# Norm sums and products on GpSimd, second block's head outputs moved by DMA, last projections in four banks

## What is computed

```python
h = _layer_norm(x, scale, offset)              # over the 512 columns
qh = (h @ wq + bq); kh = (ctx @ wk + bk); vh = (ctx @ wv + bv)      # 16 heads of 128
kh, vh = concatenate([kh, bias_k]), concatenate([vh, bias_v])       # 361 keys + 1
weights = softmax(qh @ kh.T / sqrt(128)); x = x + (weights @ vh) @ wo + bo
...
x = x + gelu(_layer_norm(x) @ w_fc1 + b_fc1) @ w_fc2 + b_fc2        # 512 -> 2048 -> 512
```

## Time and profile before

| | |
|---|---|
| median of 3 runs | 2356.04 us (2351.41 to 2356.37) |
| the profiled execution | 2354.95 us, span 2353.2 us |
| busy share of the span | PE 94%, PE weight load 92%, DVE 69%, ACT 51%, POOL 37% |
| granted TensorE clock, mean | 0.978 |
| first block's attention | about 0 to 1662 us of the span |
| its MLP | about 1662 to 1823 us |
| second block's attention | about 1823 to 2197 us |
| its MLP | about 2197 to 2353 us |

### The profile page before, as it was taken

The page is one execution under the profiler, slowest core; times in us unless marked ns, Lnnn a source line. Parts: engine busy times, 40 slices in busy tenths (PEclk is TensorE's granted clock), DMA queues, the critical chain, the costliest instruction groups (busy, mean ns, idle before and its releaser), DMA issues.

```text
span 2353.2 us, 37111 instructions
## 1 busy us (share of the span) xinstructions
PE 2219.7 (94%) x12712; PEld 2154.2 (92%) x12712; DVE 1635.1 (69%) x3781; ACT 1189.4 (51%) x2902; POOL 874.2 (37%) x854
## 2 busy tenths in 40 slices
PE   6999989999998999999899999989999899888899
PEld 5999989999998999999899999988898788877899
DVE  7777777776777777777777777766464776677543
ACT  4545554554555455554554555544232576576332
POOL 4324323242431414334142432413799112211487
PEclk9999999999999999999999999999999999999999
DMA  3646545554554546455454555534444211100143
GB/s 131 139 83 146 106 99 98 116 122 101 131 111 87 129 86 146 101 111 133 76 123 82 147 107 116 121 73 77 125 113 121 72 46 56 46 20 19 50 122 112
DMA packets 127255, 235.40 MB, mean 100 GB/s; under 512 B 22753, under 2 KB 64865, under 8 KB 127073
## 3 DMA queue, kind: packets, MB, share of 16 engines
q1 hardware_dynamic: 127072, 233.03, 44.4%
HBM read 214.96 MB, written 4.92 MB: 93 GB/s over the span
## 4 chain that ended last, share of the span: by engine, by line
PE 74%; DVE 13%; ACT 4%; POOL 4%; issue 3%; DMA 1%; SPq 0%; DVEq 0%; POOLq 0%; ACTq 0%
PE bank L693 71%; PE bank L765 2%; POOL mring L650 2%; DVE U L1294 2%; DVE ctxN L1298 1%; POOL mring L648 1%; PE bank L951 1%; DVE pT L1298 1%; ACT qT L1077 1%; DVE prob L1461 1%; ACT U L1077 1%; DVE kT L1294 1%; DVE lnb L1339 1%; DVE tmp L1408 1%; DVE ctxT L1298 1%
## 5 line engine op out<-in xcount | busy, mean ns | idle before, releaser
L648 POOL TENSOR_SCALAR mring<-stage 128x512 fp32r<-128x512 f32 x325 | 229.2, 705 | 1221.2 <-PE bank L693 1077.1
L693 PE MATMUL bank<-ctxT,kring 128*128 128x362 f32 x3456 | 632.7, 330 | 3.6 <-DVE ctxT L1298 3.6
L693 PEld LDWEIGHTS bank<-ctxT,kring 128*128 128x128 f32 x3456 | 585.9, 190 | 8.6 <-POOL mring L650 3.7
L693 PE MATMUL bank<-pT,ctxN 128*128 128x400 f32 (+1 forms) x2304 | 475.3, 354 | 12.9 <-DVE U L1298 12.8
L650 POOL TENSOR_TENSOR mring<-stage,mring 128x512 fp32r<-128x512 f32 x325 | 436.3, 1343 | 27.1
L693 PEld LDWEIGHTS bank<-pT,ctxN 128*128 128x128 f32 (+1 forms) x2304 | 419.3, 192 | 14.6 <-issue 14.4
L693 PE MATMUL bank<-hT,mring 128*128 128x400 f32 x1608 | 319.1, 347 | 13.7 <-POOL mring L650 5.8
L693 PE MATMUL bank<-U,mring 128*128 128x400 f32 x1536 | 313.0, 357 | 5.6 <-POOL mring L650 3.7
L693 PEld LDWEIGHTS bank<-hT,mring 128*128 128x128 f32 x1608 | 294.6, 189 | 18.7 <-issue 8.8
L693 PEld LDWEIGHTS bank<-U,mring 128*128 128x128 f32 x1536 | 281.6, 193 | 8.8 <-POOL mring L650 5.2
L1298 DVE TENSOR_TENSOR U<-bank,U 128x400 fp32r<-128x400 f32 x256 | 146.0, 572 | 172.6 <-ACT U L1077 172.6
(11 more groups left out here) (90 smaller groups left out, 2973.5 us busy)
## 6 DMA issues: line engine op xcount, KB each, us to landing
ctxT_raw<-in_ctx SPq DMA_DIRECT2D x72, 724.0 KB, 7.4
ctxN_raw<-in_ctx SPq DMA_DIRECT2D x256, 192.0 KB, 3.1
stage<-in_wk SPq DMA_DIRECT2D x64, 256.0 KB, 4.3
stage<-in_wq SPq DMA_DIRECT2D x64, 256.0 KB, 2.7
stage<-in_wv SPq DMA_DIRECT2D x64, 256.0 KB, 3.7
stage<-in_wo SPq DMA_DIRECT2D x64, 256.0 KB, 2.7
stage<-in_fa SPq DMA_DIRECT2D x64, 256.0 KB, 2.7
stage<-in_fb SPq DMA_DIRECT2D x64, 256.0 KB, 2.6
```

The costliest lines, as they stand in the source:

```text
L648: nc.gpsimd.tensor_scalar(hi, src, 1.0, 1.0, ALU.mult, ALU.mult).then_inc(S.w_hi, 1)
L693: mm = pe.matmul(dst, parts_l[a], parts_r[b], start=first and k == 0, stop=last and k == len(order) - 1)
```

## The change

- Norms 1 to 4, 7 and 8: the two sums go to POOL, as does the product with the reciprocal; the product with the column scale goes to ACT (`norm_scale` there). Differences, squares, high and low parts are cut into two pairs of chunks and put in neighbouring steps; the reciprocal is cut into halves of 200 columns. The norm then ends at n0+9 instead of n0+6. (For norm 7, the first sum stays on DVE.)
- Norm 0: PE adds the four chunks itself in `first_mean` and `first_var`.
- Second attention: `value_sum1_high` and `value_sum1_low` copy the whole bank, 128 x 400, into `heads_out` (the buffer of the second query tile), and SP moves it to `attnT` with four DMAs (`save_heads`). ACT waits for them (`at_in`) before it writes `heads_out` again, and `project1` waits for them. The queries of half 1 use one buffer and come a step later.
- The last group's projections use four banks (`o_bank`), with no wait for x between them; `up(1)` comes ahead of them, and in the second MLP ahead of `project1`.
- The four "1v" tiles are loaded by DMAs of their own and split by ACT and DVE in F = 13 to 17.

```diff
-        add(275 + 6 * j, "1v", j)
         add(T_MLP[0] + NF - 1 + j // 2, "1q", j)
         add(303, "1k", j)
-        add(T_ATT1 + 9 + j, "1c", 0, j)
+        add(T_ATT1 + 10 + j, "1c", 0, j)
         add(T_ATT1 + 29, "1c", 1, j)
...
-IN_W1 = {("a", 1): 0, ("b", 0): 1, ("a", 2): 2, **{("1v", j): j for j in range(4)},
-         **{("1c", 1, j): j for j in range(4)}}
+IN_W1 = {("a", 1): 0, ("b", 0): 1, ("a", 2): 2, **{("1c", 1, j): j for j in range(4)}}
...
+BY_POOL = [1, 2, 3, 4, 7, 8]
...
-        attnT = qT
+        attnT, heads_out = qT, qs[1]
 
         bank = [ctx.enter_context(nc.psum_tensor(f"bank{i}", [P, 512], F32)) for i in range(8)]
         M_BANK, T_BANK = 5, 4
         U_BANK = [6, 7]
         V_BANK = [5, 6, 7, 5]
+        O_LAST = [5, 6, 7, 4]
...
+        def qs_of(Q):
+
+            if Q < 4:
+                return Q % 2, 32 * (Q // 2)
+            return 0, 64 + 32 * (Q - 4)
+
+        def o_bank(G, c):
+            return bank[O_LAST[c] if G == GN - 1 else M_BANK]
...
         APPLIED = [[], [], [0, 1, 2], []]
-        S_CPROJ, CPROJ = NS // 2 + 3, [[0], [1], [2, 3], []]
-        S_Q1 = 8
+        S_CPROJ, CPROJ = NS // 2 + 3, [[], [0], [1, 2, 3], []]
+        S_Q1 = 9
...
+            def save_heads(t):
+
+                b, j = divmod(t, 4)
+                sp.wait_ge(S.y_lo, t + 1)
+                for i in range(HG):
+                    r, a = slice(i * HD1, (i + 1) * HD1), j * ROWS + b % NB * LQ
+                    sp.dma_start(f32(attnT[r, :, a:a + LQ]), f32(heads_out[r, :, i * LQ:(i + 1) * LQ]))\
+                        .then_inc(S.at_in, 16)
+
+            def load_values_weight():
+                sp.wait_ge(S.v_tmp, HG * GN)
+                sp.wait_ge(S.up_mm, 3)
+                sp.wait_ge(S.dn_mm, 1)
+                for j in range(4):
+                    sp.dma_start(w1_raw[:, j, 1, :], T["1v"][j]).then_inc(S.v1w_in, 16)
 
...
+            def norm_sum(li):
+                half = norm_half(li)
+                pool.wait_ge(*x_complete(li))
+                if lnb_free(li):
+                    pool.wait_ge(*lnb_free(li))
+                dst = lnb[:, 0, :]
+                nc.gpsimd.tensor_tensor(dst, x_c(half, 0), x_c(half, 1), ALU.add).then_inc(S.ln_sum, 1)
+                for c in (2, 3):
+                    pool.wait_ge(S.ln_sum, 3 * li + c - 4)
+                    nc.gpsimd.tensor_tensor(dst, dst, x_c(half, c), ALU.add).then_inc(S.ln_sum, 1)
+
+            def norm_square_sum(li):
+                k = norm_buffer(li)
+                dst = lnb[:, 1, :]
+                pool.wait_ge(S.ln_sq, DC * li + 2)
+                nc.gpsimd.tensor_tensor(dst, ln_q[k][:, 0, :], ln_q[k][:, 1, :], ALU.add).then_inc(S.ln_ss, 1)
+                for c in (2, 3):
+                    pool.wait_ge(S.ln_sq, DC * li + c + 1)
+                    pool.wait_ge(S.ln_ss, 3 * li + c - 4)
+                    nc.gpsimd.tensor_tensor(dst, dst, ln_q[k][:, c, :], ALU.add).then_inc(S.ln_ss, 1)
+
+            def norm_scale(li):
+                k = norm_buffer(li)
+                pool.wait_ge(S.ln_rstd, 2 * li + 2)
+                for c in range(DC):
+                    y = ln_c[k][:, c, :]
+                    pool.wait_ge(S.ln_cs, DC * BY_POOL.index(li) + c + 1)
+                    nc.gpsimd.tensor_tensor(y, y, lnb[:, 1, :], ALU.mult).then_inc(S.ln_y, 1)
+
+            extra = [(due, 3, convert_mask, b) for b, due in enumerate(MASK_DUE)]
+            extra += [(T_ATT1 + 4 * (b - 1) + 0.5, 2, second_context, b) for b in range(2, BATCH)]
+            for n0, li in LN_GROUP.items():
+                extra += [(n0 - 6.5, 0, norm_sum, li), (n0 + 2.5, 0, norm_square_sum, li), (n0 + 6.5, 0, norm_scale, li)]
+            s7, s8 = T_ATT1, T_ATT1 + S_CPROJ
+            extra += [(s7 + 0.9, 0, norm_square_sum, 7), (s7 + 4.5, 0, norm_scale, 7), (s8 + 0.9, 0, norm_sum, 8),
+                      (s8 + 4.6, 0, norm_square_sum, 8), (s8 + 8.6, 0, norm_scale, 8)]
+            extra.sort(key=lambda e: e[:2])
             done = 0
             for j in range(len(JOBS)):
...
+            def first_mean():
+                pe.wait_ge(S.x_in[0], 16)
+                for c in range(DC):
+                    mm = pe.matmul(bank[M_BANK][:, 0:ROWS], mean_w[:], x_c(0, c), start=c == 0, stop=c == DC - 1)
+                mm.then_inc(S.ln_mean, 1)
+
+            def first_var():
+                for c in range(DC):
+                    pe.wait_ge(S.ln_sq, c + 1)
+                    mm = pe.matmul(bank[T_BANK][:, 0:ROWS], mean_w[:], ln_q[0][:, c, :], start=c == 0, stop=c == DC - 1)
+                mm.then_inc(S.ln_var, 1)
+
...
-                    elif h == 0:
+                    elif h == 0 and G < GN - 1:
                         pe.wait_ge(S.x_add, DC * G + c)
-                    mm = split_mms(bank[M_BANK][:, 0:ROWS], w_cols(key, c), [v_out(p_, h) for p_ in range(2)],
+                    elif h == 0 and c == DC - 1:
+                        pe.wait_ge(S.pt_lo, NU)
+                    mm = split_mms(o_bank(G, c)[:, 0:ROWS], w_cols(key, c), [v_out(p_, h) for p_ in range(2)],
                                    h == 0, h == HG - 1)
...
+                if n == NU + 6:
+                    up(1)
...
-                    if F + 1 < NF:
+                    if 1 <= F < NF - 1:
                         up(NF * m + F + 1)
-                    elif m == 0:
...
+            def norm_scale(li, chunks=range(DC)):
+
+                k = norm_buffer(li)
+                for c in chunks:
+                    act.wait_ge(S.ln_sq, DC * li + c + 1)
+                    nc.scalar.activation(ln_c[k][:, c, :], ln_c[k][:, c, :], ACT.Identity,
+                                         scale=col_c(norm_cols(li)[0], c)).then_inc(S.ln_cs, 1)
+
             def norm_std(li):
...
-                b, j = divmod(s, 4)
                 act.wait_ge(S.a_mm, s + 1)
-                for i in range(HG):
-                    r, a = slice(i * HD1, (i + 1) * HD1), j * ROWS + b % NB * LQ
-                    high(attnT[r, 0, a:a + LQ], bank[A1_BANK][r, i * LQ:(i + 1) * LQ],
-                         cols[r, col["L1_xattn_v_b"] + j:col["L1_xattn_v_b"] + j + 1]).then_inc(S.a_hi, 1)
+                if s:
+                    act.wait_ge(S.at_in, 64 * s)
+                else:
+                    act.wait_ge(S.qs_out[1], 64)
+                high(heads_out[:, 0, :], bank[A1_BANK][:, 0:ROWS], col_c("L1_xattn_v_b", s % 4)).then_inc(S.y_hi, 1)
+
+            def value_weight_high(j):
+                act.wait_ge(S.v1w_in, 64)
+                high(w1[:, j, 0, :], w1_raw[:, j, 1, :]).then_inc(S.v1w_hi, 1)
 
             def context_high(i):
...
                 if norm_at(n, 1):
-                    norm_square(norm_at(n, 1))
+                    norm_square(norm_at(n, 1), (0, 1))
+                if norm_at(n, 2):
+                    norm_square(norm_at(n, 2), (2, 3))
                 if norm_at(n, 3):
                     norm_std(norm_at(n, 3))
-                if norm_at(n, 5):
-                    norm_high(norm_at(n, 5))
+                    norm_scale(norm_at(n, 3))
+                if norm_at(n, 7):
+                    norm_high(norm_at(n, 7), (0, 1))
+                if norm_at(n, 8):
+                    norm_high(norm_at(n, 8), (2, 3))
...
+                    if m == 0 and F in range(13, 17):
+                        value_weight_high(F - 13)
...
-                if s == 3:
-                    norm_high(7)
+                if s == 2:
+                    norm_scale(7)
+                if s == 5:
+                    norm_high(7, (0, 1))
+                if s == 6:
+                    norm_high(7, (2, 3))
...
+                if s == S_CPROJ + 4:
+                    norm_square(8, (2, 3))
                 if s == S_CPROJ + 6:
                     norm_std(8)
-                if s == S_CPROJ + 8:
-                    norm_high(8)
+                    norm_scale(8)
+                if s == S_CPROJ + 9:
+                    norm_high(8, (0, 1))
+                if s == S_CPROJ + 10:
+                    norm_high(8, (2, 3))
             gelu_high(NF)
...
-            def norm_rstd(li):
+            def norm_rstd(li, parts=(0, 1)):
                 dve.wait_ge(S.ln_std, li + 1)
-                nc.vector.reciprocal(lnb[:, 1, :], lnb[:, 0, :]).then_inc(S.ln_rstd, 1)
+                for k in parts:
+                    a = slice(k * ROWS // 2, (k + 1) * ROWS // 2)
+                    nc.vector.reciprocal(lnb[:, 1, a], lnb[:, 0, a]).then_inc(S.ln_rstd, 1)
...
-            norm_sum(0)
+            dve.wait_ge(S.x_in[0], 16)
+            norm_centre(0)
             context_low(0, 0)
-            norm_centre(0)
             context_low(0, 1)
-            norm_square_sum(0)
...
-                if norm_at(n, 0):
-                    norm_sum(norm_at(n, 0))
                 if norm_at(n, 1):
-                    norm_centre(norm_at(n, 1))
+                    norm_centre(norm_at(n, 1), (0, 1))
                 if norm_at(n, 2):
```

(26 more changed lines are left out.)

169 lines of the change are left out of this document (83 added, 86 removed).

## The result

The changed kernel takes 2339.0 us (median; 2332.0 to 2342.8). Beside runs of the kernel before on the same chip the ratio is 0.9925, interval 0.9907 to 0.9942: 17 us faster, where 69 were forecast. The profiled execution took 2342.8 us, its span is 2341.0, so the two traces differ by 12.2 us.

The account below looks back on a forecast made before the run. PE bounds the kernel, so time comes only from its waits and lost clock. Norms 1 to 4 35, norm 0 3, last projections 4.5, first MLP 5, second attention 21.5: 69 off 2354.95 gives 2286 us; range 2260 to 2325.

Parts of the forecast that it names:

- Norms 1 to 4, 35 us: First block's norms: 2.9 and 2.3 us from two PE waits plus 3.6 of clock, 8.8 us a norm, times 4.
- The first wait: At n0+3 PE waits 3.20 us for DVE to clear a bank after the square sums; 2.9 us saved.
- the second wait: At n0+6 PE waits 5.12 us for a key's low part on DVE; 2.3 us saved, about 2.8 stays.
- The lock: POOL work slows DVE operations with two SBUF inputs at n0+2 to n0+8; up to 2 us on the second wait.
- the rival that POOL takes back what DVE gains: Norms 1 to 4: second wait stays at 5 us with its clock; 12 us instead of 35, 2309 us; chance 0.22.
- Clock, 3.6 a norm: Norms 1 to 4: of 5 to 6 us per norm lost to PE's lower clock, 3.6 taken back.
- Second attention, 21.5 us: Second block's attention: 8 plain steps, 11 long waits, 4.5 clock, -2 new waits; bounds 0 and 33.
- The 8 us of plain steps: Second attention: a dozen plain-step PE waits sum to 11 us; whole-bank evacuation saves 8.
- The 11 us for the long waits: Second attention: six long PE waits behind DVE norm work sum to 17 us; 11 saved.
- the ring of the head rows: Second attention: copies, DMA issues and landing on single `heads_out` take 6.5 us against a step of about 7; fits narrowly.
- both rivals on it: Ring near step length: attention brings nothing, 2306 us, chance 0.08; ring longer than the step: 2406 us, chance 0.05.
- The third rival: Head-row ring near the step's length costs 1 us in most steps, attention brings nothing: 2306 us; chance 0.08.

Follow-up runs that it names:

- run 7: Changed kernel with the second block's value outputs evacuated in pieces as before, straight into attnT, no row transfers: 2344.8 us, attention 378.8.
- run 8: Changed kernel with SP issuing the value outputs' rows ahead of the queries' and masked queries' transfers of the same step: 2331.6 us, ratio 0.9903, attention 362.5.
- run 9: Changed kernel with norms 7 and 8 as before the change: 2332.2 us, attention 365.5; with norm 8 alone as before: 2334.6 us, attention 368.2.
- run 1: Changed kernel with norms 1 to 4 back on DVE at the old steps: 2339.3 us.
- Run 4: Changed kernel with norms 1 to 4's reciprocal halves moved from steps 4 and 5 to 6 and 7, products and splits two to three steps later: 2331.7 us.
- run 2: Changed kernel with POOL's sum over x of norms 1 to 4 due at n0-0.5 instead of n0-6.5: 2325.3 us, ratio 0.9878.
- run 10: Changed kernel with run 5's pacing and run 8's order together, and the sum over x spread over three steps: 2296.4 us, ratio 0.9744.
- run 11: Run 10's kernel with norms 7 and 8 as before the change, so no norm has anything on POOL: 2294.0 us, ratio 0.9741.
- run 5: Changed kernel with norms 1 to 4 all on DVE, in small pieces paced over other steps, nothing on POOL: 2310.2 us, ratio 0.9812.

## Why the prediction was wrong

The range ended at 2260 and 2325; the time is 14 us outside. By its own steps:

- **Norms 1 to 4, 35 us: measured 0.** (The same norm code in runs 7, 8 and 9 costs 40.7 to 41.2 us for norms 1 to 3 together, the changed kernel 42.4, the old code 42.4 before and 42.2 in run 1; so all four gave about 2 us at most.) The first wait was to lose 2.9 us and lost 1.2; the second was to lose 2.3 and lost 1.1. Both steps of the text count work that leaves DVE in several steps against a wait that one step makes.
  - "In all it has 3.6 us less to do before the bank is wanted": seen from the end of PE's matmuls ahead of the wait, DVE was through with the context's low part 1.1 us sooner, not 1.8 or more. Then 0.9 came (differences of 1.04 us where sums of 1.93 stood), and 0.60 went to a new wait for ACT, which does two squares before the high part of the key (324.12 and 325.62).
  - "What stands before the key's low part falls from 4.91 to 2.64 us" is the step that failed first for the second wait. In n0+5 the half reciprocal took the products' place, 1.40 us for 2.27, and a wait of 0.69 for ACT went; but the columns of kT took 0.82 us beside POOL's products, 0.17 before. What the other half saved in n0+4, 1.25 us, didn't arrive: `normalise` took 1.40 us there, 0.60 before. It began 0.09 us behind a weight split of POOL, which both kernels have at this place and which before was nearly through. The rest went with a start of DVE 0.35 us later against PE. Run 4 has neither halves nor POOL's products in these steps, and the wait is 0.36.
- **The lock was priced at the wrong place.** The text took the steps n0+2 to n0+8 and gave the collision at most 2 us; on the second wait the norm's own POOL work cost 0.65. It cost 2.02 us and its clock at n0-11, 14 us over the four norms (run 2). The operation is `norm_sum`, whose due step n0-6.5 was read as a time; POOL has nothing to wait for there and runs it right behind the o tiles. Even the rival that POOL takes back what DVE gains kept 12 us.
- **Clock, 3.6 a norm: none came back.** At norm 1 PE's busy time over two plain groups (2 x 97.0 us) was 7.0 us before and 6.05 after, of which 1.7 are the mean matmuls: 5.3 lost to the clock, then 4.4. Norm 2 lost 1.5 us more than before and norm 3 0.3 more. With the longest wait at 1.6 us nearly all of it came back (run 10, norm 1: waits 2.4 us over plain groups, matmuls 1.7, 0.35 left of 4.45).
- **Norm 0, 3 us: measured about 0.** The first piece starts at 120.0 to 124.0 us in 13 executions with the new start, 121.4 on the mean, and at 121.6 and 121.8 in two with the old.
- **Last projections, 4.5 us: measured 7.5** (table and run 1), right in kind and above its bound of 6.
- **First MLP, 5 us: measured 3.9**, POOL's 6.0 us of waits are gone; those for `part`, 2.9 us in three before, are 4.5 in four.
- **Second attention, 21.5 us: measured 4.4**, the 2.2 us of moved work included. The 8 us of plain steps hold in kind: their waits of 1.03 are 0.39 (1976.61, 2006.20) or gone. What the new evacuation brought net of its own waits is 6 us (run 7). The 11 us for the long waits failed: in pieces and on two more engines norms 7 and 8 made new ones, and the intervals with norms 7 and 8 are shorter with both undone (run 9). "ACT can wait a microsecond or two" for the rows was 7.1 us in two waits, 4.2 us of time (run 8). The projection at the end, whose cover was "even", waits 0.84 us for the rows, and the one at s = 19, put one head later, waits 2.91.

What was right: the ring of the head rows fits the step (0.6 + 0.6 + 2.5 of issue + 1.9 of landing is 5.6 us, for 6.5 forecast; in plain steps ACT doesn't wait for it), so both rivals on it fell; the direction; and where the second wait stands. The third rival's 2306 should be 2286 + 21.5 = 2307.5, which changes nothing.

Open: whether the shared form would do as well as DVE alone if both its places were put right, the sum over x as in run 2 and the reciprocal as in run 4, since no run has the two together; what of the 2 us between runs 10 and 11 is norm 7 and what norm 8; and how much of the clock's dip in the last 28 us of the attention is chance.

## What to carry to other kernels

Before moving work off an engine that others wait for, look whether its order is at fault: the same work in small pieces, in the steps where it has room, cost a third of what it cost in lumps, or shared with another engine in the steps chosen here. A due step bounds only when work may start in a queue, so for each moved piece look up what really stands before it and what runs beside it at that time. Where one engine's work stretches another's, as POOL's did DVE's, look at the longest operations beside the moved piece at its real time. Saved work counts against a wait only as far as nothing else between the two makes the engine wait. In a DMA queue put first what an engine's single buffer waits for.

## Hardware, unexpected

- POOL's 128x400 add with both inputs in SBUF stretched DVE's 128x724 operation with two SBUF inputs from 0.90 to 1.75 us, and two of 128x400 from 0.87 to 1.27 us each (0.59 alone; a weight split ran beside the first). DVE operations with one SBUF input were stretched as well: 100x362 `normalise` from 0.41 to 1.19 us beside a product of POOL and to 1.40 beside a split, and the 128x2 column from 0.17 to 0.54 beside the adds and to 0.82 beside the products.
- TensorE's granted clock fell to its lower level behind the waits of 2.01, 2.39 and 4.05 us in the changed kernel's norm 1, but not behind each wait of that length: behind 2.02 us in run 4 the same 18 matmuls took 3.52 us where they took 5.06 in the changed kernel. In the stretches with norms 1 to 3 of runs 5 and 10, whose longest wait is 1.6 us, it was 1.00. In the second attention's last 28 us it was 0.76 and 0.94 in two executions of the same code.
- Four transfers of 25 KB take SP 2.5 us to issue, so their place in its queue weighs more than their landing.
- One execution of run 11 took 5536 us: each matmul of 362 columns took 668 ns instead of 329, from start to end, at a granted clock of 1.00. Its four others lay at 2292.8 to 2298.1. No run explains it.
